# Two lanes of a 12-stage decoder: the first lane is issued eight slots ahead of the second

## What is computed

```python
x = x + l0_attn(layernorm(x))            # attention, 16 heads, top-k queries
x = x + l0_xattn(layernorm(x), ctx)      # cross attention
x = x + l0_ffn(layernorm(x))             # 2 x (windowed attention of 8 heads, GELU gated mlp)
x = x + l1_attn(layernorm(x))            # attention of 16 heads
x = x + l1_xattn(ctx, ctx, layernorm(x))
x = x + l1_ffn(layernorm(x))             # 8 experts, top 2, 2 rounds
x = x + l2_attn(layernorm(x))            # compressed + selected + windowed attention
x = x + l2_xattn(layernorm(x), ctx, mask)
x = x + l2_ffn(layernorm(x))             # 8 adapters, top 2
x = x + l3_attn(layernorm(x))            # selective state-space scan
x = x + l3_xattn(layernorm(x), ctx)      # differential attention, 16 heads
x = x + l3_ffn(layernorm(x))             # ternary weights, 8-bit activations
```

## Time and profile before

| | us |
|---|---|
| median of 3 runs | 2965.06 |
| lowest, highest | 2959.48, 2975.03 |
| the profiled execution | 2968.52 |
| its span, from first to last instruction | 2966.7 |
| mean granted TensorE clock over the span | 0.812 |

### The profile page before, as it was taken

One profiled execution on the slowest core, in us unless ns is written; L12 is line 12 of the kernel. 1 busy time (PEld: TensorE's weight loads), 2 busy tenths in 40 slices (PEclk: granted clock), 3 DMA queues, 4 the chain that ended last, 5 costly groups with the idle time before them and its releaser, 6 DMA issues. The chain is left out here.

```text
span 2966.7 us, 33877 instructions
## 1 busy us (share of the span) xinstructions
PE 2182.5 (74%) x12457; PEld 1268.5 (43%) x12466; DVE 1714.7 (58%) x4146; ACT 1037.4 (35%) x2040; POOL 591.1 (20%) x492
## 2 busy tenths in 40 slices
PE   4778999899987878789898556557855545666753
PEld 2445656566553232257676445434412212233331
DVE  5555646454554343343536765764479879865557
ACT  0223737264554243334332222222144244232331
POOL 0003020211110010010001432420025235243430
PEclk7788999899997585679997767666669879887775
DMA  3000000000001000000000000000000000000000
GB/s 131 1 1 14 1 1 1 1 1 1 1 12 68 1 1 1 1 11 1 1 1 9 1 1 1 1 1 1 1 0 0 0 0 0 0 1 1 1 1 15
DMA packets 5667, 21.07 MB, mean 7 GB/s; under 512 B 971, under 2 KB 3583, under 8 KB 5119
## 3 DMA queue, kind: packets, MB, share of 16 engines
q1 hardware_dynamic: 5503, 18.92, 1.7%
HBM read 17.87 MB, written 1.05 MB: 6 GB/s over the span
## 5 line engine op out<-in xcount | busy, mean ns | idle before, releaser
L459 POOL TENSOR_SCALAR lane_vare<-lane_mv 128x4 f32<-128x4 f32 x64 | 15.8, 247 | 1529.6 <-DVE lane_mv L453 1529.6
L2102 PE MATMUL lane_banks<-l_attn_lane_hc,base 128*128 128x512 f32 x256 | 137.3, 662 | 115.1 <-DVE l_attn_lane_hc L2257 115.1
L2250 DVE TENSOR_TENSOR_SCAN l_attn_lane_h<-l_attn_lane_da,l_attn_lane_u 128x512 f32<-128x512 f32 x128 | 193.4, 1550 | 32.9 <-ACT l_attn_lane_da L2161 27.6
L2184 POOL TENSOR_TENSOR l_attn_lane_u<-l_attn_lane_xp,l_attn_lane_bn 128x512 f32<-128x512 f32 x128 | 153.4, 1219 | 206.9 <-ACT l_attn_lane_bn L2154 206.9
L1707 PE MATMUL lane_banks<-base,l_attn_lane_sc 128*112 128x128 f32 x256 | 56.4, 360 | 137.9 <-POOL l_attn_lane_sc L1812 99.6
L1304 ACT ACTIVATE l_attn_lane_ex<-lane_banks 128x256 f32<-128x256 f32 (+3 forms) x128 | 87.3, 703 | 185.1 <-PE lane_banks L1255 185.1
L979 ACT ACTIVATE f_attn_lane_a<-lane_banks,f_attn_lane_nmx,f_attn_lane_sq 128x192 f32<-128x192 f32 (+1 forms) x256 | 125.5, 496 | 70.0 <-DVE f_attn_lane_nmx L1059 69.2
L1468 PEld LDWEIGHTS lane_banks<-weights,l_ffn_lane_hT 128*128 128x128 f32 x1024 | 123.6, 193 | 31.8 <-issue 26.0
L1492 ACT ACTIVATE l_ffn_lane_hT<-lane_banks,weights 128x512 f32<-128x512 f32 x128 | 88.0, 687 | 140.3 <-PE lane_banks L1449 140.0
L1541 DVE SCALAR_TENSOR_TENSOR l_ffn_lane_eo<-lane_banks,l_ffn_lane_sel,l_ffn_lane_eo 128x128 f32<-128x128 f32 x224 | 63.0, 344 | 121.1 <-PE lane_banks L1468 121.1
L1468 PE MATMUL lane_banks<-weights,l_ffn_lane_hT 128*128 128x128 f32 x1024 | 126.4, 278 | 8.3 <-DVE l_ffn_lane_eo L1541 7.1
(11 more groups left out here) (517 smaller groups left out, 5357.5 us busy)
## 6 DMA issues: line engine op xcount, KB each, us to landing
weights<-packed SPq DMA_DIRECT2D x1, 5479.0 KB, 22.3
weights<-packed SPq DMA_DIRECT2D x1, 2320.0 KB, 8.2
weights<-packed SPq DMA_DIRECT2D x1, 2091.0 KB, 12.8
out<-x SPq DMA_DIRECT2D x4, 256.0 KB, 2.2
weights<-packed SPq DMA_DIRECT2D x1, 960.5 KB, 4.5
weights<-packed SPq DMA_DIRECT2D x1, 897.0 KB, 10.4
weights<-packed SPq DMA_DIRECT2D x1, 838.0 KB, 14.0
early<-packed SPq DMA_DIRECT2D x1, 792.0 KB, 8.6
```

The costliest lines, as they stand in the source:

```text
L2102: pe.matmul(ps(2 + c), w("ident"), hc[:, c, :], start=(n == 1), stop=(n == NS)).then_inc(*s.up("state_added"))
L2184: g.tensor_tensor(u[:, i % 3, :], dtx[:, c, :], bn[:, n % 2, :], ALU.mult).then_inc(*s.up("u_ready"))
L2250: v.tensor_tensor_scan(h[:, c, :], da[:, i % 3, :], u[:, i % 3, :], 0.0, ALU.mult, ALU.add).then_inc(*s.up("scanned"))
```

## The change

`run_lanes` no longer takes both lanes in turn. It counts the slots issued of each lane and gives lane 0 the next slot as long as it has issued fewer than lane 1's count plus `LEAD` = 8; otherwise lane 1. So lane 0's first 8 slots are issued alone; then slot j of lane 1 and slot j + 8 of lane 0 follow each other (634 pairs), and when lane 0 has no slot left, lane 1's last 11 slots are issued alone, which is its whole last l3_ffn unit. With `prepare`, lane 1 is then 11 slots behind lane 0 in the same stage, where it was 3 before. The rounds of the loop go from 645 to 653. The instructions, waits and DMAs of the units stay the same; only their order between the lanes differs, and with it the table loads that the compiler puts in.

```diff
--- before.py
+++ after.py
@@ -2723,6 +2723,9 @@
     return [body(eng) for body, eng in zip(bodies, engines.values())]
 
 
+LEAD = 8
+
+
 def run_lanes(net, plans):
 
     nc = net.nc
@@ -2730,17 +2733,22 @@
     over = object()
     left = [list(units) for units in plans]
     running = [None, None]
-    while any(left) or any(running):
-        for i, ln in enumerate(net.lanes):
-            if running[i] is None and left[i]:
-                seg, make, args, row = left[i].pop(0)
-                running[i] = start_unit(net, ln, engines, seg, make, args, row)
-            if running[i]:
-                ended = [next(program, over) is over for program in running[i]]
-                if all(ended):
-                    ln.finished += 1
-                    running[i] = None
-
+    slots = [0, 0]
+
+    def waiting(i):
+        return left[i] or running[i]
+
+    while waiting(0) or waiting(1):
+        i = 0 if waiting(0) and (slots[0] < slots[1] + LEAD or not waiting(1)) else 1
+        ln = net.lanes[i]
+        if running[i] is None:
+            seg, make, args, row = left[i].pop(0)
+            running[i] = start_unit(net, ln, engines, seg, make, args, row)
+        slots[i] += 1
+        ended = [next(program, over) is over for program in running[i]]
+        if all(ended):
+            ln.finished += 1
+            running[i] = None
 
 def build(nc, x_in, ctx_in, ctxT_in, mask_in, packed, out, where, pieces):
     net = Net(nc, where, pieces)
```

## The result

The changed kernel takes 3130.37 us (median of 4, 3129.62 to 3141.46) where before took 2962.27 in the same comparison: 1.057 of it, with a 95% interval of 1.053 to 1.061. A second comparison gave 1.052 (1.050 to 1.055). So the change costs 168 us by the first comparison and 155 by the second; I had forecast +30, and my dearest rival +95. The direction held and the size didn't.

The account below looks back on a forecast made before the run. TensorE bounds the feed-forward stages, VectorE l3_attn, chains of hand-overs the other attention stages. Terms 18 + 12 + 10 − 8 + 6 − 8 = +30 on the profiled 2968.5, or 2995 us on the median's scale; range 2922 to 3060.

Parts of the forecast that it names:

- my dearest rival: Whole run: chains of unlike slots add, each of 61 units paying 1.1 us more; +65 on the forecast, 3060; chance 0.20.
- the 7.75 us bubble: l3_attn: a scan's wait for ScalarE's Exp (`da`), queued behind the other lane's prelude activations; 7.75 us.
- l0_ffn, +12: l0_ffn: a 40-slot period goes from 155 to 158 us, +3 in each of four; low −32, high +30.
- D: l0_ffn: each of 24 added table loads also drains, a further 1.4 us; +33 on the forecast, 3028; chance 0.05.
- l1_attn, +10: l1_attn: lane 1's prelude runs beside lane 0's slots 11 to 21, steady part unchanged; +10 us (0 to +20).
- l2_attn, −8: l2_attn: groups beside a light prelude get shorter, light slots elsewhere cost some back; −8 us (−22 to +8).
- l1_ffn and the light stages, 0: l1_ffn (TensorE 94% full, even slots), the cross attentions priced as unchanged and l2_ffn: 0 each.
- l3_attn, +6: l3_attn: more scans wait behind preludes, less idle time where preludes met, scans themselves unchanged; +6 us (−15 to +25).
- l3_xattn, −8: l3_xattn: POOL bursts come next to each other, six-slot cycle 29.5 us, −2.4 in four cycles; −8 us (−20 to +20).
- Head and tail: Lone slots at start (+31) and end (+23) less eight saved pairs (−36): +18 us (+5 to +30).
- rival B: Light slots fill the full engine's idle time in l0_ffn and l3_attn: −43, about 2922; chance 0.20.
- A: Whole run: the rival that chains of unlike slots add, 3060, the upper end of the range; chance 0.20.

Follow-up runs that it names:

- lead4: The changed kernel with a lead of 4 slots in place of 8, lane 1 seven slots behind in the same stage: 3002.7 us, 1.011 of before.
- same_slot: Against before, lane 1 runs three slots ahead by count, so both lanes do the same slot of the same stage together: 2985.4 us, 1.005 of before.

## Why the prediction was wrong, point by point

- **The rule for a round.** I priced a round as the larger of the fullest engine's sum and the longer chain, and gave the rival that chains add 0.20, at +65. It is the rule that failed, with lone lengths measured afterwards as well: it gives +28 from the order alone, as I forecast, where +162 was measured. Unlike rounds cost up to nearly the sum of the lone lengths (9.4 of 10.1 in l3_attn, where the rule gives 7.9), and they went from 24 to 52 in f0_attn, 10 to 30 in l3_attn, 12 to 34 in l3_xattn. I had the 7.75 us bubble in hand and took it for an exception. By stage this is shown for l0_ffn and l3_attn only.
- **l0_ffn, +12.** It is +69.5. Of it 9 to 14 are the added loads, 13 to 17 contention, and 41 the rest, which is queueing between the lanes with TensorE's longer busy time in it (14 of lane 0's 40); that the rest is queueing is read off the timeline, not tested by a run. A period takes 176.9 us on average where before's four take 159.5: +17.4, and I had +3. My three Gelu rounds were priced at 5.3 and took 5.8; the larger miss is in the rounds of an Exp slot beside a prelude slot, 5.0 each. I had priced the lone Exp slot well, at 3.0 against 2.9.
- **Contention** had no term. Before had no row that shows it in l0_ffn, since its order never puts L1052 beside GpSimd's sum. A bound would have come from asking which pairs of VectorE and GpSimd work meet for the first time, and its size from l3_attn, where before's trace does have such pairs: 110 of its 128 scans run beside a GpSimd instruction and take 1.61 us on average, the other 18 take 1.20.
- **The clock.** I named a falling clock in l0_ffn as what would make me wrong upwards: it fell from 0.97 to 0.92, in l3_attn from 0.84 to 0.73. TensorE's busy time rose by 87 us over the run for the same work, and by my rule the slower instructions make up 53 of the 162 us. Whether the clock fell because of the idle gaps isn't shown. It moves without them too: four kernels with the same order in l1_attn have 0.65 to 0.72 there, and the stage takes 397 to 412 us.
- **Table loads.** 69, and 24 more in l0_ffn: right. D (a drain after each) is out by the timeline. In l0_ffn they cost 9 to 14 us, where I had counted 4 × (4.8 + 1.3) = 24.
- **l1_attn, +10:** +23.7, with +20 as my high end; among the kernels with this order it is +13 to +28, by the clock. **l2_attn, −8:** +3.2, inside its bounds; VectorE's and the chains' gains beside light slots didn't come. **l1_ffn and the light stages, 0:** +16.7 and +16.0. A stage whose slots are even isn't indifferent to the offset; l2_xattn's slots now stand beside l2_attn's and l2_ffn's long ones.
- **l3_attn, +6:** +27.2, or +16 against the slower traces of the same stage in the order of before. The sign I read off was right: VectorE's wait for `da` ahead of the scans went from 27.6 us in 8 waits to 71.0 in 22 (I had said near 80). What I set against it, the idle time regained where preludes had met, did not show. The wait in the change:

```profile
DVE l_attn_lane_h L2250 <- ACT l_attn_lane_da L2161: 71.0, 22, 8.9
```

- **l3_xattn, −8:** +22.7. The cycle went where I said and further: 24 to 30 us, 26.4 on average, where I had 29.5 (and between the two `weigh`s of the earlier trace rows lie 31.75, not the 31.9 that I read). What failed is that I put the prelude at nothing: 14 us more a unit, 28 a stage. The same slots in lead4 don't show that the bursts are what shortened the cycle.
- **Head and tail.** Lane 0's first 8 slots alone took 30.0 us where I had 31, lane 1's last unit 28.5 where I had 31. But the start gained 23.5, against my 0 for l0_attn. That isn't rival B: with no unlike pair at all, in same_slot, the start is as short (202.5), and at 15 slots it is long again (221.1). It is before's own offset that is dear here (its round of slots 6 + 3 takes 10.8 us with TensorE 5.4 and VectorE 5.1 busy in it); which pairs make it so wasn't looked into.
- **The range** ended at A's own value. I had bounded each stage from its neighbours and let their errors cancel, while the rule left the same thing out of most of them: only the start came out well below its term. That the sign was right is no credit to the terms, since four of the five stages that I priced lie above their own high ends.

## What to carry to other kernels

When two independent streams are interleaved by hand in in-order queues, price a pair of unlike steps between the larger of both and the sum of their lone chains until a trace shows which (here 5.0 us between 4.7 and 5.7 in one stage, 9.4 between 7.9 and 10.1 in another), and get the lone lengths from a run that issues the streams one after the other. Price the first slots of a unit by name too: here they cost more than the cycles gained. The offset between the streams is a setting of each stage: measure two or three offsets over the whole kernel, read the stages, and choose per stage (here 2.4% under before, where one offset for all cost up to 6.6%). And list which operations of VectorE and GpSimd, and which table functions, become neighbours for the first time.

## What the hardware showed

A VectorE `tensor_scalar` from SBUF to SBUF of 0.31 us took 0.96 us on average, up to 1.35, while GpSimd added two 128x512 tensors. Some stages repeat to 0.1 us between kernels that differ only ahead of them (l2_attn is 406.1 or 406.2 in five traces with the lead of 8), which makes a table by stage worth reading. Others don't: in the same five traces l1_attn takes 397 to 412 us, with the granted clock, and l3_attn in the order of before takes 426 to 438. And TensorE's granted clock in l0_ffn was 0.97 where it idled for 49 of 638 us, and 0.92 where it idled for 91 of 708.
